# One more block of table rows moved from GpSimd's gathers to single-row fetches on ScalarE's queue, with a hint on the loops' back edge

## The reference

```python
x = emb[item_seq]; mask = item_seq != 0
def step(h, inp):
    x_t, m_t = inp
    mx = x_t @ W + b_i
    mh = h @ U + b_r
    z = sigmoid(mx[:, :D] + mh[:, :D])
    r = sigmoid(mx[:, D:2*D] + mh[:, D:2*D])
    hh = tanh(mx[:, 2*D:] + r * mh[:, 2*D:])
    h = where(m_t[:, None], z * h + (1 - z) * hh, h)
out = softmax(h_last @ Wout + bout)
```

## Time and profile before

| | |
|---|---|
| timed runs | 1031.76, 1031.94, 1032.1 us; median 1031.94 |
| the profiled execution's own time | 1033.86 us |
| its span, first to last instruction | 1032.0 us |
| mean granted clock of TensorE | 0.989 of full speed |
| busy: PE, DVE, POOL, ACT | 979.4, 789.6, 764.2, 588.3 us |
| DMA | 185 MB, mean 179 GB/s |

### The profile page before, as it was taken

One profiled execution on the slowest core, in us unless ns is written; L12 is line 12 of the kernel. 1 busy time (PEld: TensorE's weight loads), 2 busy tenths in 40 slices (PEclk: granted clock), 3 DMA queues, 4 the chain that ended last, 5 costly groups with the idle time before them and its releaser, 6 DMA issues.

```text
span 1032.0 us, 20728 instructions
## 1 busy us (share of the span) xinstructions
PE 979.4 (95%) x5218; PEld 765.4 (74%) x5218; DVE 789.6 (77%) x2075; ACT 588.3 (57%) x1301; POOL 764.2 (74%) x805
## 2 busy tenths in 40 slices
PE   5999999999899989998999899999989999989887
PEld 4556888777677777776777777777768777766665
DVE  3444667888788878887888788788878888877777
ACT  2334555666566656665666566566656666655555
POOL 5677777777777777777777777777777777777774
PEclk9999999999999999999999999999999999999999
DMA  9997555555555555555555555555555555555553
GB/s 355 410 368 284 147 165 161 162 162 161 164 161 162 161 162 161 161 163 160 163 161 161 163 159 163 161 162 163 161 163 161 161 161 162 164 160 163 161 158 107
DMA packets 62715, 184.98 MB, mean 179 GB/s; under 512 B 16767, under 2 KB 20538, under 8 KB 62602
## 3 DMA queue, kind: packets, MB, share of 16 engines
q0 software_dynamic: 48448, 147.18, 49.3%
q1 hardware_dynamic: 12758, 35.83, 9.1%
q10 hardware_dynamic: 1396, 0.91, 0.3%
HBM read 157.78 MB, written 26.07 MB: 178 GB/s over the span
## 4 chain that ended last, share of the span: by engine, by line
PE 75%; POOL 11%; issue 6%; DMA 3%; DVE 2%; ACT 1%; SPq 0%; DVEq 0%; POOLq 0%; ACTq 0%
PE bank L470 20%; PE bank L476 13%; PE bank L472 13%; PE bank L458 12%; POOL arena L376 11%; PE bank L464 6%; PE bank L392 5%; DMA rows<-arena 2%; PE bank L439 1%; PE bank L444 1%; PE bank L440 1%; DVE h L647 1%; PE bank L397 1%; ACT cand L578 1%; DVE rh L642 1%
## 5 line engine op out<-in xcount | busy, mean ns | idle before, releaser
L376 POOL DMA_INDIRECT arena<-table,row_table x731 | 692.9, 948 | 223.1 <-issue 216.3
L576 ACT ACTIVATE bank<-bank,b_gates 128x256 f32<-128x256 f32 x400 | 179.5, 449 | 255.4 <-PE bank L476 255.4
L470 PE MATMUL bank<-h,U_sb 128*128 128x256 f32 x800 | 274.4, 425 | 18.6 <-DVE h L647 18.6
L657 DVE SCALAR_TENSOR_TENSOR bank<-bank,cand 128x256 f32<-128x256 f32 x400 | 172.8, 432 | 120.6 <-ACT cand L578 118.3
L578 ACT ACTIVATE cand<-pre,bi 128x256 f32<-128x256 f32 x400 | 202.9, 507 | 101.7 <-DVE pre L651 101.1
L458 PE MATMUL bank<-ident,arena 128*128 128x128 f32 x1496 | 228.2, 275 | 14.7 <-DMA arena<-table,row_table 14.4
L476 PE MATMUL bank<-h,U_sb 128*128 128x256 f32 x800 | 241.5, 384 | 0.0
L472 PE MATMUL bank<-h,U_sb 128*128 128x256 f32 x800 | 239.8, 381 | 0.0
L642 DVE SCALAR_TENSOR_TENSOR rh<-bank,br,r 128x256 f32<-128x256 f32 x400 | 193.6, 484 | 55.9 <-ACT r L574 33.4
L458 PEld LDWEIGHTS bank<-ident,arena 128*128 128x128 f32 x1496 | 184.9, 142 | 64.7 <-DMA arena<-table,row_table 31.4
L574 ACT ACTIVATE r<-bank,b_gates 128x256 f32<-128x256 f32 x400 | 189.9, 475 | 16.3 <-PE bank L470 14.4
(11 more groups left out here) (61 smaller groups left out, 248.4 us busy)
## 6 DMA issues: line engine op xcount, KB each, us to landing
arena<-table SPq DMA_DIRECT2D x2176, 1.5 KB
table<-arena SPq DMA_DIRECT2D x24, 768.0 KB, 4.9
arena<-table,row_table POOLq DMA_INDIRECT x731, 3.2
arena<-in_L_rec_emb SPq DMA_DIRECT2D x12, 512.0 KB, 10.3
rows<-arena SPq DMA_DIRECT2D x12, 512.0 KB, 10.7
raw<-rows,row_table POOLq DMA_INDIRECT x52, 4.7
seq<-in_r_item_seq ACTq DMA_DIRECT2D x1, 400.0 KB, 10.4
table<-arena SPq DMA_DIRECT2D x2, 192.0 KB
```

The costliest lines, as they stand in the source:

```text
L376: pool.indirect_dma_start(ring_rows(s, k), None, table, bass.IndirectOffsetOnAxis(row_table[:, t, k:k + 1], 0)).then_inc(s_slot[s][c], 16)
L470: pe.matmul(reset_sum[c], U_sb[:, D:2 * D], h[c][:, :], start=False, stop=True, skip_group_check=True).then_inc(s_reset[c], 1)
L576: act.activation(update_sum[c], update_sum[c], ACT.Sigmoid, bias=b_gates[:, 0:1]).then_inc(s_z[c], 1)
L657: dve.scalar_tensor_tensor(out=update_sum[c], in0=update_sum[c], scalar=1.0, in1=cand[c][:, :], op0=ALU.subtract, op1=ALU.mult).then_inc(s ...
```

## The change

Block 3 of slot 0 gets a third kind of fetch from turn 1 on (in turn 0 POOL still gathers it). POOL skips it in turns 1 to 8. ACT fetches its 128 rows, one DMA each, during steps 1 to 20 of the turn before. Every second step, behind chain 0's r, ACT loads the next 12 or 16 offsets into registers (10 loads a turn: 16, 16, then eight of 12). In each half step it issues a row behind r, one behind z, and one behind tanh; in the first four steps two behind tanh. PE waits for these rows on a semaphore of their own. The list of offsets grows from 17 to 25 columns, SP lays a third line of it, and DVE writes a small tile once so that the new semaphore starts at 1. The loops of PE, ACT and DVE are made with `hint_back_edge=True`.

```diff
+ACT_SLOT = (0, 3)
+    PAIRS = (16, 16) + (12,) * 8
 def over_table_steps(eng, one_turn):
-            with eng.Fori(0, TURNS - 1) as turn:
+            with nc.Fori(0, TURNS - 1, engines=[eng.engine], hint_back_edge=True) as turn:
 # SP
+            sp.dma_start(slow_line[2:3, P:(TURNS + 1) * P], slow_turned[2 * TURNS + 1:3 * TURNS + 1, :]
+                         ).then_inc(s_slow_line, 16)
 # POOL
+            pool.tensor_scalar(slow_offsets[:, 2 * TURNS + 1:3 * TURNS + 1],
+                               row_f[:, ACT_SLOT[1], RAW + ACT_SLOT[0] + RING:STEPS:RING], float(ROW_BYTES), None,
+                               ALU.mult).then_inc(s_offsets, 1)
-                        if (s, k) in SLOW:
+                        if (s, k) in SLOW or (s, k) == ACT_SLOT and n >= RING:
                             continue
 # PE, transpose_rows
+                        elif n == 0 and (s, k) == ACT_SLOT:
+                            pe.wait_ge(s_act_rows, turn * (P * 16) + 1)
 # ACT (gates split into reset, update, candidate)
             def one_turn(turn, steps):
+                first = 0
                 for s in range(steps):
                     t = RAW + turn * RING + s
+                    i = s - ACT_SLOT[0] - 1
+                    pair = PAIRS[i // 2] if steps == RING and 0 <= i < 2 * len(PAIRS) else 0
+                    def fetch(c, j):
+                        todo = ((0,), (1,), (2,)) if pair == 12 else ((0,), (1,), (2, 3))
+                        for p in todo[j] if pair else ():
+                            p += (pair // 2) * (i % 2) + (pair // 4) * c
+                            fetch_row(act, 2, first + p, offset[p]).then_inc(s_act_rows, 16)
                     for c in BOTH:
-                        gates(t, c)
+                        reset(t, c)
+                        if pair and c == 0 and i % 2 == 0:
+                            offset = load_offsets(act, 2, turn + 1, first, pair)
+                            if i == 0:
+                                act.wait_ge(s_free[1], turn * RING + ACT_SLOT[0] + 1)
+                        fetch(c, 0)
+                        update(t, c)
+                        fetch(c, 1)
+                        candidate(t, c)
+                        fetch(c, 2)
+                    if pair and i % 2 == 1:
+                        first += pair
+            act.wait_ge(s_slow_line, 16 * (len(SLOW) + 1))
+            for q in range(AHEAD):
+                act.wait_ge(s_store[q], 16 * table_stores(q))
+            act.wait_ge(s_padrow, 16 * 2)
             over_table_steps(act, one_turn)
 # DVE
+            dve.memset(inv_total[:, :], 0.0).then_inc(s_act_rows, 1)
```

More of the change, by code:

```diff
@@ L52, in gru @@
     LEFT = STEPS - RAW - TURNS * RING
-    assert SLOW[0][0] < LEFT <= SLOW[1][0]
+    assert ACT_SLOT[0] < SLOW[0][0] < LEFT <= SLOW[1][0]
+    PAIRS = (16, 16) + (12,) * 8
+    assert sum(PAIRS) == P and ACT_SLOT[0] + 2 * len(PAIRS) < RING
     BOTH = range(len(CHAINS))
@@ L115, in gru @@
         row_table = sb("row_table", [P, STEPS, BLOCKS], I32)
-        slow_offsets = sb("slow_offsets", [P, 2 * TURNS + 1])
-        slow_turned = sb("slow_turned", [2 * TURNS + 1, P], I32)
-        slow_line = sb("slow_line", [len(SLOW), (TURNS + 1) * P], I32)
+        slow_offsets = sb("slow_offsets", [P, 3 * TURNS + 1])
+        slow_turned = sb("slow_turned", [3 * TURNS + 1, P], I32)
+        slow_line = sb("slow_line", [len(SLOW) + 1, (TURNS + 1) * P], I32)
         copy_i = sb("copy_i", [P, 1], I32)
@@ L184, in gru @@
         s_slow_line = sem("slow_offsets_on_one_partition")
+        s_act_rows = sem("act_rows_fetched")
         s_slow = [sem(f"slow{b}_rows_fetched") for b in range(len(SLOW))]
@@ L225, in fetch_row @@
         def fetch_row(eng, b, p, offset):
-            return eng.dma_start(ring_rows(*SLOW[b])[p:p + 1, :].bitcast(U8),
+            return eng.dma_start(ring_rows(*(SLOW + (ACT_SLOT,))[b])[p:p + 1, :].bitcast(U8),
                                  table_bytes[:, bass.ds(offset, ROW_BYTES)])
@@ L277, in _ @@
             sp.wait_ge(s_padrow, 16 * 2)
-            sp.wait_ge(s_slow_line, 16 * len(SLOW))
+            sp.wait_ge(s_slow_line, 16 * (len(SLOW) + 1))
             def slow_block(b, turn):
@@ L345, in _ @@
                                    ).then_inc(s_offsets, 1)
+            pool.tensor_scalar(slow_offsets[:, 2 * TURNS + 1:3 * TURNS + 1],
+                               row_f[:, ACT_SLOT[1], RAW + ACT_SLOT[0] + RING:STEPS:RING], float(ROW_BYTES), None,
+                               ALU.mult).then_inc(s_offsets, 1)
             pool.tensor_copy(row_table[:, :, :], row_f.rearrange("p k t -> p t k")).then_inc(s_idx, 1)
             pool.wait_ge(s_idx, 8)
[L348 removed]
+            pool.wait_ge(s_offsets, len(SLOW) + 1)
             pool.wait_ge(s_pins, 2)
@@ L419, in _ @@
                 project(i)
-            slow_bank = bank[1][0:2 * TURNS + 1, 0:P]
-            pe.wait_ge(s_offsets, len(SLOW))
+            slow_bank = bank[1][0:3 * TURNS + 1, 0:P]
+            pe.wait_ge(s_offsets, len(SLOW) + 1)
             pe.wait_ge(s_tdve, CHUNKS + 1)
@@ L450, in transpose_rows @@
             def transpose_rows(turn, s, c):
-                gathered = sum((s, k) not in SLOW for k in CHAINS[c])
-                pe.wait_ge(s_slot[s][c], (turn + 1) * (16 * gathered) + (32 if s < RAW else 0))
+                gathered = sum((s, k) not in SLOW + (ACT_SLOT,) for k in CHAINS[c])
+                more = (32 if s < RAW else 0) + sum(16 for k in CHAINS[c] if (s, k) == ACT_SLOT)
+                pe.wait_ge(s_slot[s][c], (turn + 1) * (16 * gathered) + more)
                 for i, k in enumerate(CHAINS[c]):
@@ L570, in turned_x, with reset, update, candidate @@
                 act.copy(xT[c][:, :], x_sum[c]).then_inc(s_xT[c], 1)
-            def gates(t, c):
+            def reset(t, c):
                 act.wait_ge(s_reset[c], t + 1)
                 act.activation(r[c][:, :], reset_sum[c], ACT.Sigmoid, bias=b_gates[:, 1:2]).then_inc(s_r[c], 1)
+            def update(t, c):
                 act.wait_ge(s_update[c], t + 1)
                 act.activation(update_sum[c], update_sum[c], ACT.Sigmoid, bias=b_gates[:, 0:1]).then_inc(s_z[c], 1)
+            def candidate(t, c):
                 act.wait_ge(s_pre[c], t + 1)
                 act.activation(cand[c][:, :], pre[c][:, :], ACT.Tanh, bias=bi[:, 2:3]).then_inc(s_tanh[c], 1)
+            def gates(t, c):
+                reset(t, c)
+                update(t, c)
+                candidate(t, c)
             for t in range(RAW):
@@ L588, in one_turn @@
             def one_turn(turn, steps):
+                first = 0
                 for s in range(steps):
                     t = RAW + turn * RING + s
-                    for c in BOTH:
-                        gates(t, c)
+                    i = s - ACT_SLOT[0] - 1
[5 more added lines that the diff above has]
+                            fetch_row(act, 2, first + p, offset[p]).then_inc(s_act_rows, 16)
+                    for c in BOTH:
+                        reset(t, c)
+                        if pair and c == 0 and i % 2 == 0:
[3 more added lines that the diff above has]
+                        fetch(c, 0)
+                        update(t, c)
+                        fetch(c, 1)
+                        candidate(t, c)
+                        fetch(c, 2)
[5 more added lines that the diff above has]
+            act.wait_ge(s_padrow, 16 * 2)
             over_table_steps(act, one_turn)
@@ L632, in _ @@
             dve.wait_ge(s_slow_turned, 1)
-            dve.tensor_copy(slow_turned[:, :], bank[1][0:2 * TURNS + 1, 0:P]).then_inc(s_slow_copied, 1)
+            dve.tensor_copy(slow_turned[:, :], bank[1][0:3 * TURNS + 1, 0:P]).then_inc(s_slow_copied, 1)
             dve.wait_ge(s_params, 16 * 5)
```

## The result

| | before | changed |
|---|---|---|
| timed runs, median | 1032.02 us (1031.76 to 1032.72) | 1046.19 us (1044.57 to 1047.63) |
| ratio to before | | 1.0135, interval 1.0122 to 1.0147 |
| profiled span | 1032.0 us | 1044.4 us |
| table gathers on POOL, the last starts at | 731, 1019.6 us | 723, 1007.9 us |
| one turn of the loop, DVE's branch to its branch | 98.8 to 101.6 us | 101.6 to 101.9 us |

What follows compares the result with a forecast made beforehand. POOL's gathers were taken as the bound: 1026.6 - 10.0 = 1016.6 us, later than the recurrence's 988 + 2 + 18 = 1008, giving span 1022.0 and median 1021.9. The range was 1020.5 to 1036, the forecast's own part 1020.5 to 1023.5.

Steps and rivals of the forecast that it cites:

- The two paths and their bound: Kernel end: the later of POOL's gathers (1016.6 us) and the PE, ACT, DVE recurrence (1008) counts, so POOL's.
- The hint: Loop back edges: DVE's stall falls from 3.3 us to 0.3, six times; with clock falls gone, 21 us off the recurrence.
- Two rows behind tanh: ACT, tanh to r in the first four steps: r 0.25 us late, 2.0 us a turn, 16 us in eight turns.
- The step that failed: ACT, r to z: proportional loads of 0.76 and 1.02 us, mostly absorbed before tanh; about 2 us in all.
- the prediction's slack of 0.22: ACT's idle time between z and tanh, 0.22 us, taken to absorb z's lateness after a load.
- signs that the prediction itself named for being wrong: PE never waiting for gathers at the end; ACT loads over 0.9 us for 12; row issues well over 0.25; 3 us branch gap.
- Rival A: ACT's queue becomes the bound, offset loads having a fixed share: chance 0.16 slower, 0.02 near old, 0.19 between that and forecast.
- the point of decision: ACT's loads: 8.6 us of reserve over 80 loads, 0.11 us a load above proportional.
- SP: SP's row fetches stay off the path: 17 blocks, 49 us each, some 50 with waits, done near 949; 985 needed.
- rival C: ACT's and SP's row issues share a unit: SP's blocks take 54.5 us, end at 1025, time near 1060; chance 0.04.
- the reserve between them: Kernel end: POOL's path at 1016.6 us against the recurrence at 1008, 8.6 us in reserve.

Runs made afterwards that it cites:

- both moves: Changed kernel, same pairs: only the load behind r in a load's half step, no second row behind tanh, displaced rows behind the other r's; 1022.57 us, ratio 0.9900.

## Why the prediction was wrong

**The two paths and their bound: right.** The gathers went to 723 and the last one started at 1007.9 (1009.5 forecast; the pitch was 1.251). The hint alone leaves the time at 1031.86. With the recurrence out of the way the kernel takes 1022.57 and 1022.83, where the prediction put POOL's path at 1021.9.

**The hint: right in its main part.** 0.3 us at the branch, 96.3 us a turn. What was missed: a stall soon after the hinted loops are left. It appears in the changed kernel (ACT 2.08 at 897.56, DVE 1.76 at 912.90), in the run with the hint alone (DVE 3.3 us, 24 us behind its last branch at 863.8), and in the one with both moves (ACT 3.4 us, 10 us behind its last branch, DVE 1.8 us, 27 behind). The traces tie it to the hint: DVE has one stall of this kind, starting 24 to 30 us behind its last branch, in all ten kernels with the hint and in none of the four without. ACT has one, 10 to 15 us behind its last branch, in the eight hinted kernels in which it fetches rows. SP shows it too once its loop is hinted (the distance of 15.4 us above). In the changed kernel both lie on the path; the time from DVE's last branch to the end is some 2 us longer for them.

**Two rows behind tanh: right, a little low.** 0.25 us was forecast, though the prediction's own terms, 0.64 + 0.07 - 0.42, make 0.29 and not 0.27. r stands 0.67 behind tanh in one chain and 0.73 or more in the other, and moving six of the rows gave 1.8 us a turn, 0.3 each.

**The step that failed: "With its row and 0.07, z comes 0.06 and 0.32 late, and ACT idles 0.22 before tanh, which absorbs that. Cost 0.1 us for each of the 16 loads of 16, about 2 us."** Two numbers in it were too small. The load is dearer than in proportion: 0.96 us for 12 and 1.20 for 16, where proportion gave 0.76 and 1.02 (the line through the two is 0.24 + 0.06 n). And the first row behind a load is issued in 0.46 us, not 0.23; the trace of the kernel before could not show this, since SP's first issues take 0.26. Together they are 0.41 to 0.43 us more in a gap that was already full by the prediction's own count, with z 0.06 and 0.32 late. z came 0.55 and about 0.85 us late, and the gap before tanh made good 0.30 of that (the prediction's slack of 0.22 was not the error).

The bill: where the prediction gave 0, a load of 12 costs 0.26 a time on average, 64 x 0.26 = 17 us. A load of 16 comes on top of two rows behind tanh and costs 1.73 - 4 x 0.28 = 0.6, 16 x 0.6 = 10 us, where it gave 2. The second rows cost 64 x 0.28 = 18 us where it gave 16. With 2 us of a later loop start (174.4 against 172.5) and some 2 us of the stalls in turn 7 the excess is 17 + 8 + 2 + 2 + 2 = 31 us, and the recurrence ended at 1039.1 instead of 1008. The later loop start is not the change's: the 14 profiled executions enter the loop either at 172.5 to 172.9 or at 174.2 to 174.6, with and without rows on ACT. Two of the signs that the prediction itself named for being wrong are there: loads of over 0.9 us for 12, and row issues well over 0.25 us.

Rival A named the mechanism and the point of decision (0.11 us a load) but priced only a fixed share, and so that a load of 32 stayed at 2.03. At 0.4 us fixed a load of 12 was 0.25 dearer, z 0.31 late, and 11 us in all; measured, z is 0.55 late. The long first issue is the difference. A result slower than before by this way had 0.16.

**SP: wrong, without consequence for the changed kernel.** The prediction had SP done near 949. The earlier trace rows already speak against that: SP's last load starts at 962.2, and its last row leaves at 974.8 in the kernel before. It is done at 983.0 in the changed kernel, since a block takes 50.9 us (50.6 before, where the prediction counted 49 to 50) and SP's own back edge 2.5 to 3.3 a turn. In the profiled execution of the kernel with both moves this was the bound.

**Two issuers hamper each other (rival C): not so.** SP's row issue is 225 ns at the median with and without ACT's, at most 330 against 327 in the changed kernel; a block of SP takes 50.9 us against 50.6, 1%. Single issues grew longer in later runs, up to 0.67 us, but at most 7 of the 2108 that do not stand behind a load went over 0.3 in any run. The exclusive lock of the Trainium skill (Perfetto Trace Analysis, DMA Instruction — HWDGE (DVE, Sync)) may exist, but no run here shows its price beyond that.

**What stays open.** By what mechanism the hint leaves a stall behind the end of its loop, and whether it can be avoided: no run was made on it. Why the first issue behind a load takes 0.46 us on ACT and 0.27 on SP. The spread from run to run of 5 to 8 us in the kernels whose bound is the recurrence (1024.7 to 1029.6, 1024.1 to 1029.2, 1029.7 to 1037.4) was not explained either; in the last of them the granted clock was 0.995 or 0.996 in every execution, so it is not the clock there.

## What to carry to other kernels

Work for a sequencer has to be priced gap by gap, with its fixed shares: here the same loads and the same rows cost 5.5 us a turn or 0.6, by their places alone. A run that is to isolate a part has to be looked up in its own trace: the one without rows had no loads either, and its time alone would have passed for a proof that they are free. When a change leans on two near-equal paths, the reserve between them (8.6 us here) should be held against the number of times the uncertain price is paid (80 loads, 320 half steps) before a chance is named. A path that was never the bound, such as SP's, must be counted with its back edges before it is called hidden.

## What the runs showed of the hardware

- A load of registers from SBUF took 0.96, 1.20, 1.20 and 2.04 us for 12, 13, 16 and 32 values where it started on a multiple of four 4-byte values, and 2.78, 3.0 and 3.6 to 3.7 for 12, 13 and 16 where it did not. The Trainium skill (Runtime: NRT & Kernel Launch, Instruction fetch mechanics) gives about 200 ns a register even in bulk, for loads that it describes as coming from HBM. The loads from SBUF with a start off that multiple are near it (0.23 a register), the others at a third to two fifths of it (0.06 to 0.08).
- The first DMA issue behind a load of registers took 0.46 us or a little more on ACT, also where z stood between, and 0.23 after; on SP it took 0.26 to 0.27, and 0.225 after.
- The hint takes a back edge from 3.3 to 0.3 us on DVE. On SP the time over a usual distance of loads falls from 2.4 to 3.5 us to 0.6 to 0.9. It is followed by one stall of 1.3 to 3.4 us in the code behind the loop, in every kernel that has it and in none that has not.
- ACT's loop body grew from 156 to over 430 instructions, and without the hint its back edge went from 0.3 to 2.6 us. The same section of the Trainium skill says that a taken branch waits for a fetch when its target is outside the two blocks of 256 instructions that are held. The trace agrees in part: the longer bodies stall and the short one does not, but the bodies of DVE (333) and ACT (434) are under the 512 of two blocks, so the size alone does not say which one stalls.
